# Patch arithmetic of two kinds joined, the first feed-forward pass reordered, and four row scatters issued in two pairs

## What is computed

```python
h = tokenize(x)                               # 16x16 patches: 196 tokens an image, 768 features
                                              # layernorm, @ W (768 x 192) + b, layernorm, each with gain and shift
h = h + attention(layernorm(h))               # 12 heads of 16, then a projection
h = h + block(layernorm(h)) where block(x):
    x = x + attention(ln1(x))
    x = x + gelu(x @ mlp_w1 + mlp_b1) @ mlp_w2 + mlp_b2      # 192 -> 768 -> 192
    xm = ln2(x); top 2 of 4 experts by xm @ gate_w.T + gate_b, gates = softmax of the two
    return x + sum over the chosen experts of gate * (gelu(xm @ w1[e] + b1[e]) @ w2[e] + b2[e])
```

## Time and profile before

| | |
|---|---|
| median of 3 runs | 3275.29 us |
| lowest, highest | 3263.19, 3321.31 us |
| profiled execution | 3305.81 us |
| its span, first to last instruction | 3304.1 us |
| mean granted TensorE clock | 0.948 |
| busy: TensorE, VectorE, ScalarE, GpSimd | 87%, 70%, 57%, 45% |

### The profile page before, as it was taken

How to read it: one execution, slowest core, us unless ns; L and a number is a source line. 1 busy time by engine, 2 the same in 40 slices (tenths; PEclk the granted TensorE clock), 3 DMA queues, 4 the chain that set the end, 5 groups by cost and what they waited for, 6 DMA issues and landing times. The chain is left out here.

```text
span 3304.1 us, 94922 instructions
## 1 busy us (share of the span) xinstructions
PE 2859.4 (87%) x31229; PEld 2189.6 (66%) x31229; DVE 2298.8 (70%) x5357; ACT 1870.2 (57%) x3666; POOL 1478.1 (45%) x2213
## 2 busy tenths in 40 slices
PE   4777737999999999999999986888892999999998
PEld 4777724555555555555555545788882888888887
DVE  4666636777777777777777745656653777777776
ACT  3666615666666666666666655656661444444443
POOL 3666632333333344444444311466666344444444
PEclk8888858999999999999999998999996999999999
DMA  5444324555556566666666644434332343344343
GB/s 134 128 116 129 85 57 110 148 148 148 150 148 151 150 154 169 156 164 161 161 160 161 155 107 119 125 117 129 123 120 102 63 69 65 68 67 69 66 68 49
DMA packets 514473, 393.85 MB, mean 119 GB/s; under 512 B 222433, under 2 KB 487683, under 8 KB 514179
## 3 DMA queue, kind: packets, MB, share of 16 engines
q1 hardware_dynamic: 474146, 338.79, 39.4%
q0 software_dynamic: 38496, 46.38, 7.9%
q10 hardware_dynamic: 1536, 4.82, 0.6%
HBM read 232.59 MB, written 155.42 MB: 117 GB/s over the span
## 5 line engine op out<-in xcount | busy, mean ns | idle before, releaser
L657 DVE TENSOR_REDUCE a_mx<-a_mxp 98x4 f32<-98x784 f32 x768 | 746.4, 972 | 296.2 <-PE a_mxp L806 294.1
L533 ACT ACTIVATE a_pt<-a_st 98x784 f32<-98x784 f32 x768 | 631.6, 822 | 201.2 <-PE a_st L792 199.7
L1553 POOL DMA_INDIRECT out_dram<-f_yo,f_idg x202 | 330.2, 1635 | 420.4 <-DVE f_yo L1887 386.8
L479 POOL TENSOR_TENSOR a_cn<-a_ctxs,a_rec 128x392 f32<-128x392 f32 x192 | 189.7, 1016 | 523.8 <-DMA a_rec<-a_recip 523.8
L1627 ACT ACTIVATE f_hf<-f_bank,f_b1c 128x256 f32<-128x256 f32 x606 | 253.8, 472 | 236.7 <-PE f_bank L878 236.7
L868 PE MATMUL a_pr<-a_pf,a_cn 128*98 128x192 f32 x1536 | 331.9, 346 | 7.8 <-POOL a_cn L479 4.6
L821 PE MATMUL a_pv<-a_pt,a_vp 98*32 98x196 f32 x6144 | 337.5, 337 | 0.8 <-ACT a_ctxs L564 0.5
L806 PE MATMUL a_mxp<-a_kst,a_qst 48*128 48x196 f16 x3072 | 261.4, 248 | 61.7 <-DMA a_kst<-a_qk 42.2
L2043 PE MATMUL f_bank<-f_w2h,f_hh 128*128 x1212 | 298.9, 247 | 15.2 <-DVE f_hl L1871 14.0
L2044 PE MATMUL f_bank<-f_w2h,f_hl 128*128 x1212 | 298.2, 246 | 0.0
L2045 PE MATMUL f_bank<-f_w2l,f_hh 128*128 x1212 | 298.2, 246 | 0.0
(11 more groups left out here) (306 smaller groups left out, 7878.4 us busy)
## 6 DMA issues: line engine op xcount, KB each, us to landing
a_rec<-a_recip SPq DMA_DIRECT2D x256, 147.0 KB, 3.5
t_rows<-in_x_dram SPq DMA_DIRECT2D x84, 392.0 KB, 5.7
a_qst<-a_qk SPq DMA_DIRECT2D x256, 110.2 KB, 3.2
a_kst<-a_qk SPq DMA_DIRECT2D x256, 110.2 KB, 3.0
f_xg<-f_listed SPq DMA_DIRECT2D x101, 264.0 KB
a_qk<-a_qkh SPq DMA_DIRECT2D x128, 196.0 KB, 2.6
a_qk<-a_qkl SPq DMA_DIRECT2D x128, 98.0 KB, 2.7
a_qk<-a_qkh SPq DMA_DIRECT2D x128, 98.0 KB, 2.4
```

The lines of the kernel that those rows point to most:

```text
L533: act.activation(pt[k % PT][:].rearrange("p j a t -> p j (a t)"), st_ps[0:half_t, :, 0:unit_t], ACT.Exp, scale=sm_scale).then_inc(exp_s, 1)
L657: dve.tensor_reduce(mx[:, a, :, 2 * p:2 * p + 2].rearrange("p q j -> p j q"), mx_ps[0:half_t, :, 0:unit_t].rearrange("p j (q t) -> p j q t ...
L1553: pool.indirect_dma_start(out, bass.IndirectOffsetOnAxis(ap=idg[i % 3][:, t:t + 1], axis=0), yo[i % 3][:, t, :], None, compute_op=ALU.add) ...
```

## The change

In the patch stage kind A runs one unit further ahead (unit s + 3), and GpSimd does D first and then one chain of four small operations for A and C together, on four columns, of which A's statistics fill the first two and C's the last two (`mv`, `rstd` and `shift` are shared, the latter two in three buffers). ScalarE issues the six column loads ahead of its row loads; SP's row loads of a step stand ahead of its store. In the first feed-forward pass `turn_tokens` moves from c = 2 to c = 1, `prefix` from the head of a step to c = 2, `affine_tokens` behind the first `hidden`, `low_tokens` ahead of the second `low_hidden`. GpSimd issues the scatters of tile 0 before the step's sum and root, those of tile 1 after them.

```diff
-        LAG = {"A": 2, "B": 1, "C": 0, "D": -1}
+        LAG = {"A": 3, "B": 1, "C": 0, "D": -1}
+        FIRST, NORM = -3, 4
@@ sync
-            for col, vec in ((gcol, ln1_g), (bcol, ln1_b)):
-                for c in range(chans):
-                    v = vec.rearrange("(q p c) -> c p q", c=chans, p=128)[c]
-                    sp.dma_start(col[:, c * per:(c + 1) * per], v, allow_slow_non_contiguous=True).then_inc(w_in, 16)
             for t, vec in ((bias_row, bias), (g2, ln2_g), (b2, ln2_b)):
-                sp.dma_start(t[:], vec.partition_broadcast(R)).then_inc(w_in, 16)
+                sp.dma_start(t[:], vec.partition_broadcast(R)).then_inc(row_in, 16)
             def step(s, kinds):
-                if "D" in kinds:
-                    u = s - 1
...
                 if "B" in kinds:
                     u = s + 1
...
+                if "D" in kinds:
+                    u = s - 1
...
@@ gpsimd
-                if "A" in kinds:
-                    u, b = s + 2, s % 2
-                    wait(pool, mv_s, 2 * (u + 1))
-                    wait(pool, xn_s, 2 * (u - 1))
-                    rsqrt(pool, rsqrt_s, u * RSQRT_OPS, mv[b][:, :, 1], rstd[b][:], eps[:], minus_half[:])
-                    wait(pool, rsqrt_s, RSQRT_OPS * (u + 1))
-                    pool.tensor_tensor(shift[b][:], mv[b][:, :, 0], rstd[b][:], ALU.mult).then_inc(sh_s, 1)
-                    wait(pool, sh_s, 2 * u + 1)
-                    pool.tensor_tensor(shift[b][:], shift[b][:], minus_one[:], ALU.mult).then_inc(sh_s, 1)
-                if "C" in kinds:
...
-                    rsqrt(pool, rsqrt2_s, u * RSQRT_OPS, mv2[b][:, :, 1], rstd2[b][:], eps2[:], minus_half[:])
...
                 if "D" in kinds:
...
+                if "A" in kinds or "C" in kinds:
+                    at = NORM * (s - FIRST)
+                    cs = slice(0 if "A" in kinds else 2, 4 if "C" in kinds else 2)
+                    m, r, h = mv[s % 2], rstd[s % 3], shift[s % 3]
+                    if "A" in kinds:
+                        wait(pool, mv_s, 2 * (s + 4))
+                        wait(pool, xn_s, 2 * (s + 1))
+                    if "C" in kinds:
+                        wait(pool, mv2_s, 2 * (s + 1))
+                        wait(pool, yn_s, 2 * (s - 2))
+                    pool.tensor_tensor(r[:, cs], m[:, cs, 1], eps[:, cs], ALU.add).then_inc(norm_s, 1)
+                    pool.wait_ge(norm_s, at + 1)
+                    pool.tensor_tensor(r[:, cs], r[:, cs], minus_half[:, cs], ALU.pow).then_inc(norm_s, 1)
+                    pool.wait_ge(norm_s, at + 2)
+                    pool.tensor_tensor(h[:, cs], m[:, cs, 0], r[:, cs], ALU.mult).then_inc(norm_s, 1)
+                    pool.wait_ge(norm_s, at + 3)
+                    pool.tensor_tensor(h[:, cs], h[:, cs], minus_one[:, cs], ALU.mult).then_inc(norm_s, 1)
@@ scalar
+            for col, vec in ((gcol, ln1_g), (bcol, ln1_b)):
+                for c in range(chans):
+                    v = vec.rearrange("(q p c) -> c p q", c=chans, p=128)[c]
+                    act.dma_start(col[:, c * per:(c + 1) * per], v, allow_slow_non_contiguous=True).then_inc(col_in, 16)
             for which in range(N_LOADS):
                 load(act, 0, which)
-            act.wait_ge(w_in, 16 * (KT + 2 * chans + 3))
+            act.wait_ge(col_in, 16 * 2 * chans)
+            act.wait_ge(w_in, 16 * KT)
...
-                        wait(act, sh_s, 2 * (u + 1))
+                        wait(act, norm_s, NORM * (u + 1))
...
-                wait(act, sh2_s, 2 * (u + 1))
+                wait(act, norm_s, NORM * (u - FIRST + 1))
@@ vector
+            dve.wait_ge(row_in, 16 * 3)
...
-                    wait(dve, sh_s, 2 * (u - 1))
+                    wait(dve, norm_s, NORM * (s - 1 - FIRST))
...
+                    wait(dve, norm_s, NORM * (s - 1 - FIRST))
                     wait(dve, st2_s, 2 * (u + 1))
                     dve.memset(spacer[:], 0.0)
                     for t in range(2):
-                        dve.bn_aggr(mv2[b][:, t, :], stats2[:, t, :]).then_inc(mv2_s, 1)
+                        dve.bn_aggr(mv[b][:, 2 + t, :], stats2[:, t, :]).then_inc(mv2_s, 1)
@@ feed-forward, gpsimd
             for s in range(NU + 6):
+                due = done < NU and first_unit[batch_of[done]] + sizes[batch_of[done]] - 1 <= s - 6
+                if due:
+                    scatter(done, (0,))
                 if 2 <= s < NU + 2:
                     u = s - 2
...
-                if done < NU and first_unit[batch_of[done]] + sizes[batch_of[done]] - 1 <= s - 6:
-                    scatter(done)
+                if due:
+                    scatter(done, (1,))
                     done += 1
@@ feed-forward, scalar
+                if s < NU:
+                    hidden(s, 0)
                 if 3 <= s < NU + 3:
                     affine_tokens(s - 3)
-                if s < NU:
-                    hidden(s, 0)
@@ feed-forward, vector
                     normed(s - 2)
+                if s + 1 < NU:
+                    low_tokens(s + 1)
                 if s < NU:
                     low_hidden(s, 1)
...
-                if s + 1 < NU:
-                    low_tokens(s + 1)
@@ feed-forward, tensor
-                if s - 5 in batch_end:
-                    prefix(batch_end[s - 5])
...
-                    if c == 2 and s + 1 < NU:
+                    if c == 1 and s + 1 < NU:
                         turn_tokens(s + 1)
+                    if c == 2 and s - 5 in batch_end:
+                        prefix(batch_end[s - 5])
```

## The result

The changed kernel takes **3167.14 us** (median of 4 runs, 3159.79 to 3168.45), the kernel before in the same series 3298.3 (4 runs, 3263.19 to 3344.27). The ratio is 0.9683, 95% interval 0.9643 to 0.9723: faster by 3.2%. Every ratio in this document leaves out executions that lie more than 1.5% above the fastest of the same kernel. The profiled execution took 3159.79 us.

What follows compares the result with a forecast made beforehand. Bound by a loop of waits through GpSimd in the patch stage and by TensorE in the first feed-forward pass; -85 + 3 - 36 - 2.5 = -120.5 us on 3305.8, by ratio 3156 us, range 3105 to 3222.

Steps and rivals of the forecast that it cites:

- Patch step: Patch stage, steady state: product statistics 5.2 us apart instead of 6.74, 85 us less, bounds 68 and 101.
- 4.9 us loop: Patch stage: loop closing in one step, joint chain 1.85, `yn` 0.94, D 2.03, hand-over about 0.1 us.
- two-step loop: Patch stage: `mv` 0.99, chain 1.85, `yn` 0.94, patch and transposes 3.04, products 3.4: 10.2 us, 5.1 a step.
- Beginning: Patch stage's start: first statistics at about 39 us, 3 later than before; bounds 8 earlier to 6 later.
- if it goes ahead of group 1: Start of patch stage: condition under which group 0's rows are in by 28 us, the early bound; late bound 42.
- First pass: First feed-forward pass: new order removes waits for `ml` and before prefix sums, 36 us less, bounds 15 and 54.
- in steady state four scatters stand between one root and the next sum, before and after: First feed-forward pass, GpSimd: only where a step's first two scatters fall changes; only the end gains, 2.5 us.
- Step length: First feed-forward pass: steps of about 8.6 to 8.9 us instead of 9.67.
- Tail: Behind the first feed-forward pass's last root: 34 scatters instead of 36, 2.5 us less, bounds 0 and 2.6.
- rival 2: First feed-forward pass: the order wins nothing because waits move to `hl`; -84.5 us, or 3191; chance 0.07.
- Rival 5: Patch stage: joint chain waits for the later statistics and holds ScalarE up; step 6.0, 3199 us; shared chance 0.15.
- Rival 3: Patch step stays at 6.0 us and the feed-forward order wins nothing: -43 us, or 3233; chance 0.08.

Runs made afterwards that it cites:

- patch part alone: The kernel before with everything changed in the patch stage and the first feed-forward pass left as it was: 3231.19 us, ratio 0.9837.
- the run again: The changed kernel's same code measured once more in a later series, against the kernel before: 3180.18 us, ratio 0.9670.
- without the split: The changed kernel with all four scatters together again behind GpSimd's sum and root, against the kernel before: 3211.24 us, ratio 0.9776.

## Why the prediction was right, step by step

Forecast 3156, measured 3167.14, and 3180.18 when run again; as a share, 3.65% less forecast, 3.2 and 3.3% measured. The sum came out in part by luck, as two errors went against each other: patch stage and beginning were put at 82 us and are worth 53 by the ratio of the patch part alone, the rest was put at 38.5 and is worth about 52. The two profiled executions differ by 146 us where 120.5 were forecast: patch stage and its beginning 90.5 (82 forecast), first pass 61.6 (36), tail 4.3 (2.5), the gap to the second pass 6.2, less 13.2 in attention and 3.5 in the second pass.

- **Patch step: right in mechanism, mis-sized by 0.24.** It is the 4.9 us loop, not the 5.2 between the bounds; of the earlier trace rows the 1.85 holds (1.84). The two-step loop that I put at 5.1 measures 4.8: the patch is taken up 0.80 us behind `yn`'s start, not 0.94, patch and transposes are 2.79 and not 3.04, products 3.18 and not 3.4. The clock went to 1.00. The rule of the Trainium skill (TensorE: Matmul & The Clock Gate, HAM oscillation) for waits between bursts would have given the better term. The traces agree with it only in part: the old code had 1.00 as well with TensorE busy for 39.3 of 50 us, and 0.86 when busy for 41.0. What the sum lacked: the profiled execution of before was on the long side of its own patch stage, by 44 us.
- **Beginning: wrong in size, +3 forecast, +6.9 measured**, outside my upper end of 42 by 1. The step that failed is "if it goes ahead of group 1": the two queues shared (43.0 beside group 1, 26.9 with it held back). The Trainium skill (DMA: Bandwidth & Descriptors, Queues, rings and completion order) says so, and the 41 worked out by it was nearer than my 39. Held back, the start is at 26.9, below my 28.
- **First pass: -36 forecast, -42 in the run again and -62 in the profile shown.** Right: no wait for `ml` or before the prefix sums, and the third pair's `hl` is what is late next. Wrong: "in steady state four scatters stand between one root and the next sum, before and after", taken as proof that the split does nothing there. Without it the same order gives 442.8 to 452.5. A count of instructions in a cycle says nothing of which phase the cycle settles in.
- **Step length: 8.6 to 8.9 forecast; over the last 34 steps 8.46 on average in the changed kernel and 8.87 in the run again, 8.12 at best.** I subtracted idle time from the step. But the busy time of a step holds stalls that the view does not show as idle: for the same instructions it is 8.67 us a step in the kernel before (of 9.75), 8.26 in the changed one and 8.12, the whole step, in the quickest. Differences from start to start give the floor.
- **Tail: right.** 34 behind the last root; 4.3, 2.7, 3.0 and 2.2 us in four comparisons for 2.5. With 32 it is 3.6 more.
- **Rivals.** None came about in the change itself; rival 2's `hl` takes 8.8 us of 300. Rival 5 was real and is the cost of one unit less of distance. Rival 3's sum is off by 2.5: by its own terms it is -41 + 3 - 2.5 = -40.5, not -43, or 3235.

**What stays open.** Why the slow gait lasts 9.6 us. In it VectorE and ScalarE wait for products of TensorE whose semaphores come late, up to 3.1 us behind the modelled end of their matmul. Without the split, 77 operations waited for an event over 0.3 us late, and nearly all start 0.02 us after it, so the delay is real for the readers. From 2100 to 2350 us it is 0.76 us on average without the split and 0.01 in the changed kernel's first profile, where all events are in the trace; 0.73 in the kernel before and 0.46 in the run again, where 37 of 221 and 16 of 229 are missing. It is 0.02 in attention and, in every kernel, 0.01 in the steps ahead of the first scatter. But it is 0.01 in the second pass as well, where GpSimd scatters too: scatters alone do not make it. Whether TensorE is held up there by something that the trace does not show, or only its records are early, no run here tells apart: a pass without its scatters leaves the second pass no rows, and was not tried.

## What to carry to other kernels

When a small chain on a slow engine serves two consumers of different lag, joining it saves little and ties the early one to the late one; first give the early one a whole step of distance (10.21 against 4.96 us here), then join. Take the step of a multi-engine loop from each closed path in turn, from starts to starts: paths of 4.92 and 4.8 us made a step of 4.96, and a forecast that adds a margin for the clock was 0.24 too long. Parts of a change that work on the same loop have to be tried together: here +17, -18 and -53 us alone made about -105 together. And one profile of the kernel before may be a long one: look for a second before pricing what there is to gain.

## What the runs showed of the hardware

- One piece of code, the patch stage of the kernel before, settled at 6.75 us a step with a granted clock of 0.86 to 0.90 in two executions and at 5.94 with 1.00 in a third; the changed one was at 4.96 in all nine profiles that have its patch stage whole.
- Two queues with 12 and 9 row loads shared 242 to 268 GB/s so that statistics of the group asked for first could start only when nearly all of both was in (at 43.0 us, and at 26.9 with the nine held back).
- Attention, with unchanged code, took 1602.6 to 1626.8 us in the profiles: 1.5%, so a smaller difference there between two executions tells nothing of a change.
